# A key tile's TensorE work in another order: all four scores around P times V first, then the four maxima, then both filler pieces

## What is computed

```python
x = x + 0.5 * ffn(layernorm(x), W_base, b_base, W_router, lora_A, lora_B)
x = x + attn(layernorm(x), ...)
x = x + 0.5 * ffn(layernorm(x), W_base, b_base, W_router, lora_A, lora_B)

# attn: 32 heads of 16, 8 key/value heads, weights as signs times a scale
scores = einsum('bhqd,bhkd->bhqk', q, k) / sqrt(16)
out = einsum('bhqk,bhkd->bhqd', softmax(scores), v)
# ffn: x @ W_base.T + b_base + top-2 of 8 LoRA experts of rank 16, chosen by x @ W_router.T
```

## Time and profile before

| | |
|---|---|
| time, median of 3 runs | 1253.77 us (1252.16 to 1256.37) |
| the profiled execution: its time / its span | 1249.78 us / 1248.0 us |
| PE busy | 1105.1 us (89%) |
| DVE busy | 896.8 us (72%) |
| ACT busy | 716.7 us (57%) |
| POOL busy | 277.0 us (22%) |

### The profile page before, as it was taken

How to read it: one execution, slowest core, us unless ns; L and a number is a source line. 1 busy time by engine, 2 the same in 40 slices (tenths; PEclk the granted TensorE clock), 3 DMA queues, 4 the chain that set the end, 5 groups by cost and what they waited for, 6 DMA issues and landing times.

```text
span 1248.0 us, 19266 instructions
## 1 busy us (share of the span) xinstructions
PE 1105.1 (89%) x5944; PEld 463.6 (37%) x5944; DVE 896.8 (72%) x1311; ACT 716.7 (57%) x1313; POOL 277.0 (22%) x455
## 2 busy tenths in 40 slices
PE   1867686689998999999999999999999999998847
PEld 1656564233423342323333333333233323232335
DVE  3685868877787778787778778777886797773164
ACT  2352522365776677676667566656665676667611
POOL 4142526510331042130032003100400130022010
PEclk9998888699999999999999999999999999999979
DMA  7012132211020101200200021103001200200300
GB/s 236 18 51 85 61 95 81 78 29 36 25 60 24 41 25 51 63 25 25 74 24 24 24 80 30 30 24 78 24 24 37 60 24 24 75 6 6 84 0 34
DMA packets 87331, 59.03 MB, mean 47 GB/s; under 512 B 44144, under 2 KB 73328, under 8 KB 87280
## 3 DMA queue, kind: packets, MB, share of 16 engines
q1 hardware_dynamic: 87280, 58.39, 16.2%
HBM read 37.64 MB, written 20.32 MB: 46 GB/s over the span
## 4 chain that ended last, share of the span: by engine, by line
PE 77%; DVE 15%; ACT 3%; POOL 2%; issue 1%; DMA 1%; SPq 0%; POOLq 0%; DVEq 0%
PE ps_score L1181 21%; PE ps_out L1193 20%; PE ps_max L1160 17%; PE ps_fill L1118 6%; DVE neg_max L982 4%; PE ps_fill L1145 2%; DVE neg_max L1040 2%; PE ps_fill L1091 2%; PE ps_out L1118 2%; DVE xt_l L935 1%; PE ps_fill L1122 1%; DVE zd L896 1%; DVE zm L892 1%; DVE zd L888 1%; PE ps_fill L1103 1%
## 5 line engine op out<-in xcount | busy, mean ns | idle before, releaser
L760 ACT ACTIVATE probs<-ps_score 128x512 f32<-128x512 f32 x1024 | 568.8, 596 | 297.8 <-PE ps_score L1181 291.2
L982 DVE TENSOR_REDUCE neg_max<-ps_max 128x1 f32<-128x1024 f32 x480 | 577.8, 1220 | 205.3 <-PE ps_max L1160 200.4
L1160 PE MATMUL ps_max<-kst,qst 96*128 96x512 bf16 x1024 | 389.4, 386 | 25.2 <-DVE neg_max L1040 12.8
L1181 PE MATMUL ps_score<-qst,kst 99*128 99x512 bf16 x1024 | 395.5, 388 | 13.9 <-ACT probs L760 8.2
L1193 PE MATMUL ps_out<-probs,v_ring 128*32 128x512 f32 x2048 | 273.6, 606 | 0.7 <-ACT probs L760 0.7
L1181 PEld LDWEIGHTS ps_score<-qst,kst 99*128 99x128 bf16 x1024 | 98.7, 97 | 397.3 <-ACT probs L760 347.8
L1160 PEld LDWEIGHTS ps_max<-kst,qst 96*128 96x128 bf16 x1024 | 98.8, 99 | 83.6 <-DVE neg_max L982 24.0
L307 POOL TENSOR_TENSOR wait_pad<-wait_pad 1x1 bf16<-1x1 bf16 x55 | 10.3, 187 | 437.2 <-DVE neg_max L982 363.4
L1193 PEld LDWEIGHTS ps_out<-probs,v_ring 128*32 128x32 f32 x2048 | 40.3, 108 | 107.3 <-issue 85.4
L1091 PE MATMUL ps_fill<-ident,xn 128*128 128x128 f32 x192 | 32.0, 292 | 39.3 <-ACT xn L709 25.7
L709 ACT ACTIVATE xn<-xc,ln_shift,rstd 128x512 f32<-128x512 f32 x48 | 38.1, 812 | 41.1 <-POOL ln_shift L574 41.1
(11 more groups left out here) (197 smaller groups left out, 1259.9 us busy)
## 6 DMA issues: line engine op xcount, KB each, us to landing
qst<-q_dram SPq DMA_DIRECT2D x192, 64.0 KB, 2.2
q_dram<-zm SPq DMA_DIRECT2D x24, 256.0 KB, 2.6
kst<-k_dram SPq DMA_DIRECT2D x192, 32.0 KB, 2.1
xc<-x SPq DMA_DIRECT2D x8, 512.0 KB, 3.7
x_dram<-xc SPq DMA_DIRECT2D x8, 512.0 KB, 3.1
xc<-x_dram SPq DMA_DIRECT2D x8, 512.0 KB, 4.1
out<-xc SPq DMA_DIRECT2D x8, 512.0 KB, 2.9
att_dram<-att SPq DMA_DIRECT2D x31, 128.0 KB, 2.0
```

The costliest lines, as they stand in the source:

```text
L760: act.activation(probs[:, kt % 2, j, :], ps_score[j % 2][:, :], ACT.Exp, scale=1.0 / HD ** 0.5).then_inc(probs_ready, 1)
L982: dve.tensor_reduce(neg_max[:, uu % 2, t:t + 1], ps_max[max_slot(uu, pos)][:, :, :], AXY, ALU.max, negate=True).then_inc(max_read, 1)
L1160: last = pe.matmul(ps_max[slot][:, half, :], qst[0:SR, r, j, q * P:(q + 1) * P], kst[0:SR, r, half * 512:half * 512 + 512], start=True, st ...
L1181: pe.matmul(ps_score[j % 2][:, :], kst[0:SR + PARTS, uu, kt * P:(kt + 1) * P], qst[0:SR + PARTS, uu, j, :], start=True, stop=True).then_in ...
```

## The change

Only the TensorE order inside `body` is another one. Both filler pieces of a tile and all four maxima come behind score 3, and the turn too; the wait for the next keys and queries (`qk_loaded`) moves from the start of a unit to the first maxima. No matmul is added or taken away, and the orders of the other engines stay.

```diff
-                    if kt == 0 and has_max:
-                        pe.wait_ge(qk_loaded[(uu + 2) % UB], i * 192 + 192 * ((uu + 2) // UB + 1))
                     if kt == 0:
                         pe.wait_ge(rows_loaded[uu], i * 48 + 48)
+                    pairs = [(max_use(i, uu, pos), max_slot(uu, pos), (uu + 2) % UB, t) for pos, t in max_pairs(kt)] if has_max else []
+                    score(i, uu, kt, 0)
+                    score(i, uu, kt, 1)
+                    if not (first and slot == 0):
+                        times_v(i, uu - (kt == 0), (kt - 1) % KT)
+                    score(i, uu, kt, 2)
+                    score(i, uu, kt, 3)
                     if kt == 1:
                         turn(i, uu, turn_use(i, uu, last), turn_slot(uu, last), rows=not (last and uu == 3),
                              out=not (first and uu == 0))
-                    pairs = [(max_use(i, uu, pos), max_slot(uu, pos), (uu + 2) % UB, t) for pos, t in max_pairs(kt)] if has_max else []
-                    for j in range(2):
-                        score(i, uu, kt, j)
-                        for pair in pairs[:1]:
-                            max_matmul(*pair, j)
-                    if not (first and slot == 0):
-                        times_v(i, uu - (kt == 0), (kt - 1) % KT)
-                    score(i, uu, kt, 2)
-                    for pair in pairs[1:]:
+                    if kt == 0 and has_max:
+                        pe.wait_ge(qk_loaded[(uu + 2) % UB], i * 192 + 192 * ((uu + 2) // UB + 1))
+                    for pair in pairs:
                         max_matmul(*pair, 0)
-                    for item in plan.get(2 * slot, []):
-                        fill(item)
-                    score(i, uu, kt, 3)
-                    for pair in pairs[1:]:
                         max_matmul(*pair, 1)
-                    for item in plan.get(2 * slot + 1, []):
-                        fill(item)
+                    for half in (2 * slot, 2 * slot + 1):
+                        for item in plan.get(half, []):
+                            fill(item)
```

## The result

| | before | after |
|---|---|---|
| median of the runs on the same chip | 1252.97 us (1251.5 to 1256.37, 4 runs) | 1319.34 us (1317.86 to 1323.84, 4 runs) |
| ratio to before, 95% interval | | 1.0532 (1.0498 to 1.0565) |
| profiled execution: time / span | 1249.78 / 1248.0 us | 1319.35 / 1317.5 us |

The change makes the kernel 66 us slower. The prediction had said 1300 in a range of 1277 to 1322: the direction and the range hold, and the loss is larger than the 47 us of the sum.

The account below looks back on a forecast made before the run. It took TensorE and ScalarE, waiting for each other, as the bound. Five loop passes at +6.3 (31.5), the last 0 and the first two 16 made 47 us: 1297 profiled, median about 1301, taken as 1300, range 1277 to 1322.

Parts of the forecast that it names:

- VectorE's margin: Tiles without filler: reductions end at about 4.97, the buffer is needed at 5.29; margin 0.3, less with VectorE readers to run.
- Loss 1 and 2: Pieces FFb0, Ob0, T0b, T1b wait for VectorE reads, +5.85 us a pass; HT0 waits for the `logit` copy, +1.0.
- nothing lets `xc` pass reduction a: FFb0's tile: VectorE's order is unchanged, so read `xc` stays behind pair a's reduction; the tile loses 1.52 us.
- early pair a was the cover: Attention tiles before: pair a's early place covered the VectorE reads that second pieces wait for; no size of its own.
- Loss 3: Pair b waits for the turn's reads: tiles 16 to 18 +1.24, 8 and 9 +0.53, 26 +0.60; two turns gain 0.76.
- the turn ends at 2.47, the chain at about 3.5: Tile 1, VectorE free: times of the turn and its `shift_rows`, `recip`, `att` chain; pair b 0.6 late, tile takes 3.93.
- The gain of 0.38 a turn: Tiles 0 and 1 at two turns of a pass: 7.01 us together, under the 7.22 shown; 0.38 counted for each.
- Gains: Loop pass, 2.90 us: tiles 2 to 5 0.88, 12 to 15 0.47, two turns 0.76, five other tiles 0.79.
- the rival in which VectorE becomes the bound: Margin of 0.3 too small, unfilled tiles gain nothing, 9.2 us in each of seven passes: 1318 us, chance 0.06.
- the rival that it falls: TensorE's standing still lowers the granted clock, 5.5 us in each of eight passes, 44 more: 1345 us, chance 0.06.
- unfilled tiles that win: Gains of 2.90 a pass stay and second pieces' losses shrink; 1233 us with the losses gone, chance 0.05.
- losses half hidden: Losses of the waiting pieces stand, the turn costs nothing: 3.95 a pass, 28 in all, 1282 us, chance 0.09.

Follow-up runs that it names:

- experiment 1: The changed kernel, with VectorE's readers for the filler pieces put ahead of the reduction of pair a: 1246.23 us, ratio 0.994.
- experiment 2: The kernel before, with both filler pieces and pair b behind score 3, pair a left early: 1238.11 us, ratio 0.9869.
- experiment 4: The kernel before, with score 0, both maxima of pair a and score 1 in a row: 1240.68 us, ratio 0.9893.
- experiment 7: The kernel of experiment 2, with pair a moved ahead of score 0 (at tile 1 behind it): 1222.73 us, ratio 0.9767.
- experiment 8: The kernel before, with pair a alone moved ahead of score 0 (at tile 1 behind it): 1234.8 us, ratio 0.9862.
- experiment 9: The kernel before, with VectorE's readers put ahead of the reduction of pair a: 1262.19 us, ratio 1.0076.
- experiment 10: The kernel of experiment 7, with VectorE's readers put ahead of the reduction of pair a: 1236.24 us, ratio 0.986.
- experiment 6: The changed kernel, with filler piece T1b and its VectorE read moved one line later in the list: 1309.36 us, ratio 1.0462.
- experiment 3: The changed kernel, with the turn alone put back to the head of tile 1: 1318.84 us, ratio 1.0528.
- experiment 5: The changed kernel, with each tile's first filler piece put back ahead of score 3: 1336.68 us, ratio 1.0679.

## Why the prediction was right, and where its sizes were off

**What bounds the kernel.** Right. TensorE and ScalarE form a cycle, 3.10 to 2.88 in tiles without filler, and VectorE's margin was enough in the tiles 2 to 5: none of their maxima waits. It was not in tile 14 (below).

**Loss 1 and 2, the pieces behind VectorE.** Right in mechanism and size: four second pieces 5.78 without the clock's part (forecast 5.85), HT0 1.04 (1.0). The step that nothing lets `xc` pass reduction a is shown by experiment 1, which lets it pass and takes the loss away, and the step that early pair a was the cover by experiment 2, in which the pieces are as late as in the change and cost nothing.

**Loss 3, the turn.** In part. Tiles 16 to 18 (1.28 for 1.24), 8 and 9 (0.70 for 0.53) and 26 (0.57 for 0.60) came as worked out. The two turns counted as a gain of 0.76 gave 0.30. The failed step is "the turn ends at 2.47, the chain at about 3.5": score 1 of tile 1 comes 0.46 into the tile instead of 0.22, `shift_rows` starts at 765.91 - 762.90 = 3.01 and `att` ends at 3.94. The first 0.24 only moved: the forecast had put it into tile 0 (3.08, measured 2.84). What is lost is the chain, 3.94 - 3.01 = 0.93 from `shift_rows` to the end of `att` for 0.79, and smaller steps at its two ends; together the two tiles take 7.29 for the 7.01 forecast. The gain of 0.38 a turn had no row behind it either: the turn shown gives 7.22 - 7.01 = 0.21 (the tiles 0 and 1 had taken 7.37, which would have given 0.36).

**Gains.** Tiles 2 to 5 gained 0.92 (0.88). Tiles 12 to 15 were to gain 0.47 and lose 0.07. The step that failed is the margin of 0.3 "less where VectorE has readers to run": in tile 13 a reader met POOL, took 1.07 more than its usual 0.41, and pair b of tile 14 was late by 1.01. This is the rival in which VectorE becomes the bound, in one tile of a pass.

**The clock.** This is the largest miss. The sum took the clock as unchanged ("The granted clock should stay at 1.00 in the loop"); the rival that it falls had a chance of 0.06 and 5.5 us in each pass. In the changed kernel it came in part: one fall of 1.6 in each loop pass, 8.0 in all. The first two passes and the last have such falls too: P times V takes 1.85 to 1.87 in tiles 10 and 29 of the first, 4 of the second and 8 of the last. The first two passes have the same plan, and no fall at the same tile, so each shows what the other's falls cost: tiles 10 and 29 of the first 6.66 and 4.57 for 5.02 and 3.11, 3.1 us; tiles 3 and 4 of the second 6.86 and 5.26 for 6.45 and 2.83, 2.8 us. In the last pass it is 1.6 (tiles 7 and 8, 5.37 and 4.62, for 5.06 and 3.29 in the loop). That makes an estimate of 15.5 us, by which the change without the clock would have cost about 54. The argument against the rival, that waits of up to 2.8 went by without a fall, misread its row: these are waits of weight loads, beside which matmuls still run. The matmuls themselves wait 0.6 at most in the loop of the kernel before, so nothing in that loop spoke for or against; of the two passes ahead of it, one wait of 1.92 in the second did go by without a fall.

**The sum.** A loop pass was to lose 6.3 and lost 9.1: 1.6 by the clock, 0.5 by tiles 12 to 15, 0.5 by two turns, 0.2 by tiles 8 and 9. Five passes make 14 us of the missing 22 (69.5 - 47 in the profiled executions). The first two passes lost 9.35 and 10.3 for 8 each, the second just over the range of 6.3 to 10; without the falls it is 7.5 for the second, near the forecast. The last lost 2.2, of it 1.6 by the clock, where none was counted. The remaining 2 are the later start of the attention and the shorter end. So the forecast 47 and the 54 without the clock are near each other, and the median fell inside the range, at its upper end, for a reason that the range did not name: its high end stood for VectorE as the bound. The other rivals, unfilled tiles that win (1233) and losses half hidden (1282), found nothing in the rows.

**What brings the falls.** Over all twelve kernels, the five loop passes of each (waits of TensorE's matmuls over 1.2 us, and falls, counted in the traces):

| kernels | waits over 1.2 us in a pass | falls in five passes |
|---|---|---|
| before, experiments 2, 4, 7, 8 | none | 0, 0, 0, 0, 0 |
| experiments 1, 9 | one of 1.37 to 1.39 | 0, 1 |
| experiment 10 | one of 1.77 | 2 |
| experiment 6 | three of 1.5 | 2 |
| the change, experiments 3, 5 | four of 1.5 to 1.6 | 5, 4, 2 |

Each of the 16 falls begins within 0.6 us after the end of such a wait. So the falls go with the stalls, and no kernel without stalls has one in its loop; but no experiment changed the stalls alone, and why one stall is followed by a fall and the same stall in the next pass is not stays open.

## What to carry to other kernels

Before moving an instruction on the engine that sets the pace, look at who reads its result and what stands behind that reader in its own queue: the maxima cost nothing where they went, but the read behind their reduction did, about 1.5 us each time in four tiles of a pass, and with it the next tile's scores. Test an order as a pair with the order of the engine that it talks to, since one edit to VectorE's order was worth -73, +9 and +12 us under three orders of TensorE. The best order found keeps what the change gains (four maxima between score 3 and the next score 0, filler behind score 3) and puts pair a behind the filler instead of ahead of it: 1222.73 us, 0.9767 of the time before.

## What the runs showed of the hardware

- The granted clock fell for about one tile in passes with waits of 1.4 to 1.8 us on TensorE: 0.68 over a tile in which TensorE was busy throughout. It cost 1.6 us in that pass, and about 15.5 of the changed kernel's 66 in all (an estimate from the same tiles with and without a fall). In the loop it came right behind such a wait, but behind one of several, and which one differed from pass to pass of one execution; behind the same wait of 1.77 us it came in two passes of five.
- A VectorE instruction of 0.41 us on SBUF took 0.85 and 1.48 beside POOL instructions of 0.61 and 1.26 that had started just before, and ended 0.29 after them both times. In experiment 9 a `COPY_PREDICATED` of 0.71 started 0.30 after a POOL instruction of 1.31, took 1.62 and ended 0.61 after it.
